# A causal attention block on one Trainium2 core: the table of interleaved jobs set anew, the inverses stored and spread ahead of the next stack

## The reference

```python
xn = _layernorm(x, axis=-1)
qkv = xn @ w_qkv.T + b_qkv                       # 16 heads of 16 channels
att = einsum('bhqd,bhkd->bhqk', q, k) / sqrt(16) + hope_bias(i - j, head)
att = softmax(where(causal, att, -inf))
attn = einsum('bhqk,bhkd->bhqd', att, v).reshape(B, T, C) @ w_proj.T + b_proj
ffn  = fp8_quantised(bf16(xn)) @ fp8_quantised(kernel)   # rounded to bf16, plus bias
out  = x + attn + ffn
```

## Time and profile before

| | us |
|---|---|
| median of three runs | 926.57 (926.45 to 929.19) |
| the profiled execution | 926.98 |
| its span, first to last instruction | 925.2 |
| PE busy | 811.6 (88%) |
| DVE busy | 716.6 (77%) |
| ACT busy | 574.8 (62%) |
| POOL busy | 527.2 (57%) |

### The profile page before, as it was taken

How to read it: one execution, slowest core, us unless ns; L and a number is a source line. 1 busy time by engine, 2 the same in 40 slices (tenths; PEclk the granted TensorE clock), 3 DMA queues, 4 the chain that set the end, 5 groups by cost and what they waited for, 6 DMA issues and landing times.

```text
span 925.2 us, 22869 instructions
## 1 busy us (share of the span) xinstructions
PE 811.6 (88%) x6121; PEld 497.2 (54%) x6121; DVE 716.6 (77%) x2523; ACT 574.8 (62%) x1194; POOL 527.2 (57%) x521
## 2 busy tenths in 40 slices
PE   7688888998998889899889898888989989899883
PEld 4455455554555555465556555555554555555442
DVE  4778678897877987888798887888787988879702
ACT  4256567676666757677666666766676776666550
POOL 5435538575573857556474765558375655738360
PEclk9669799998999999999999999999998999999786
DMA  5926455564655555555655565466456646646202
GB/s 150 173 62 117 88 120 117 121 126 106 128 118 127 112 115 126 120 121 121 140 108 112 114 141 122 110 128 120 109 122 121 128 108 129 122 99 120 56 31 76
DMA packets 55549, 106.08 MB, mean 115 GB/s; under 512 B 10464, under 2 KB 30432, under 8 KB 55520
## 3 DMA queue, kind: packets, MB, share of 16 engines
q1 hardware_dynamic: 55048, 105.19, 54.1%
q10 hardware_dynamic: 472, 0.54, 0.2%
HBM read 18.68 MB, written 8.91 MB: 30 GB/s over the span
## 4 chain that ended last, share of the span: by engine, by line
PE 56%; DVE 12%; SPq 10%; issue 7%; ACT 7%; DMA 6%; ACTq 1%; POOL 0%; DVEq 0%; POOLq 0%
PE misc_a L535 9%; PE misc_a L646 9%; PE misc_b L646 9%; PE misc_b L535 6%; PE scoreT_b L624 5%; PE scoreT_c L624 4%; ACT probs L879 4%; PE scoreT_a L624 4%; SPq L324 3%; DVE quant_work L997 3%; SPq L377 2%; DMA stacks<-neg_max_T 2%; SPq L371 2%; PE score_a L601 2%; DVE row_max L958 2%
## 5 line engine op out<-in xcount | busy, mean ns | idle before, releaser
L1174 POOL TENSOR_SCALAR_AFFINE_SELECT probs<-probs 128x512 f32<-128x512 f32 x256 | 166.7, 663 | 264.5 <-ACT probs L879 263.3
L958 DVE CUSTOM_DVE_ANT_0 score_b<-score_b,causal_mask_q 128x384 f32<-128x384 f32 (+3 forms) x321 | 162.0, 521 | 82.1 <-PE score_b L601 80.7
L958 DVE CUSTOM_DVE_ANT_0 score_c<-score_c,causal_mask_q 128x256 f32<-128x256 f32 (+3 forms) x384 | 169.8, 469 | 52.1 <-PE score_c L601 51.4
L879 ACT ACTIVATE probs<-scoreT_c 128x384 f32<-128x384 f32 (+1 forms) x256 | 135.1, 528 | 107.7 <-PE scoreT_c L624 52.9
L958 DVE CUSTOM_DVE_ANT_0 score_a<-score_a,causal_mask_q 128x512 f32<-128x512 f32 x319 | 172.5, 557 | 16.3 <-PE score_a L601 16.2
L879 ACT ACTIVATE probs<-scoreT_a 128x512 f32<-128x512 f32 (+1 forms) x256 | 141.4, 553 | 51.1 <-PE scoreT_a L624 36.5
L879 ACT ACTIVATE probs<-scoreT_b 128x384 f32<-128x384 f32 (+1 forms) x256 | 132.4, 517 | 31.3 <-PE scoreT_b L624 22.4
L958 DVE DVE_READ_ACCUMULATOR2_ANT row_max<- 128x1 f32 x1024 | 143.1, 140 | 0.0
L624 PE MATMUL scoreT_a<-stacks 64*128 64x512 f32 (+3 forms) x320 | 119.5, 393 | 26.6 <-DMA stacks<-neg_max_T 15.5
L624 PE MATMUL scoreT_c<-stacks 64*128 64x256 f32 (+3 forms) x384 | 123.6, 346 | 12.3 <-ACT probs L879 10.4
L601 PE MATMUL score_b<-stacks 64*128 64x384 f32 (+3 forms) x321 | 116.5, 395 | 11.1 <-DVE row_max L958 11.1
(11 more groups left out here) (234 smaller groups left out, 2019.1 us busy)
## 6 DMA issues: line engine op xcount, KB each, us to landing
stacks<-qk_parts SPq DMA_DIRECT2D x128, 512.0 KB, 8.1
x_ring<-in_L_attn_x SPq DMA_DIRECT2D x16, 512.0 KB, 3.4
attn<-out_T SPq DMA_DIRECT2D x64, 128.0 KB, 2.7
xn<-recips SPq DMA_DIRECT2D x31, 256.0 KB
out<-x_ring SPq DMA_DIRECT2D x15, 512.0 KB, 2.9
stacks<-neg_max_T SPq DMA_DIRECT2D x128, 4.0 KB
low_features<-neg_max_T SPq DMA_DIRECT2D x124, 4.0 KB
low_features<-probs SPq DMA_DIRECT2D x8, 128.0 KB, 4.1
```

Source lines behind the costliest of these rows:

```text
L879: A(probs_slot(g, k), STB[(SLOTS * g + k) % 3][:, 0:w], ACT.Exp).then_inc(exp_done, 1)
L958: last = V.tensor_tensor_reduce(bank, bank, CMQ[:, T - w:T], 1.0, LEAST, ALU.add, ALU.max, MX[:, g % 2, h, qt:qt + 1])
L1174: last = GP.affine_select(out=d, in_=d, compare_op=ALU.is_ge, fill=0.0, base=0, pattern=[[0, HU], [1, P]], channel_multiplier=-1)
```

## The change

The change edits the tables of slots, one ACT and one DVE step, one place in POOL's list and SP's list.

| job or step | before | after |
|---|---|---|
| PV (PE) | (g,3) | (g,3) |
| MT (PE), max_T (ACT) | (g,5), (g,6) | (g,3) behind PV, k = 4 behind out_T |
| QK jobs (PE) | (0,7) (0,9) (1,7) (1,11) | (0,8) twice, (1,8) twice |
| V jobs | (2,1) (2,11) | (2,6) twice |
| FF jobs | (2,7) twice | (2,9) twice |
| PJ jobs | (3,1) (3,7) | (3,6) twice |
| result (DVE) | (3,2) (3,8) | (3,6) (3,8) |
| XH (ACT) | (3,10) (3,11) | (3,9) (3,10) |
| XB (ACT) | (0,2) (0,3) | behind XH, (3,9) (3,10) |
| T_lo (DVE) | (0,0) (0,1) | (3,10) and (0,2) |
| invert (DVE) | (0,10) | (0,8) |
| attn_hi (ACT) | (2,7) (2,8) | (2,3) twice |
| quant_magic (DVE) | (2,7) (2,8) (2,9) | (2,3) (2,5) (2,6) |
| divide (POOL) | behind mask (1,2) | in front of it |

XB no longer waits for T_lo; T_lo now waits for XB, and a T bank counts as free once T_lo has read it. SP stores the inverses right behind `load_max(b, 1)` and spreads them behind the load of x, both ahead of `load_stack(b + 1, 0)`; before, the store stood behind that stack and the spread behind `load_max(b, 2)`.

```diff
-QK_AT = [(0, 7), (0, 9), (1, 7), (1, 11)]
+QK_AT = [(0, 8), (0, 8), (1, 8), (1, 8)]
...
@@ sync, body
                 load_max(b, 1)
+                if not first:
+                    store_recips(b - 1)
                 if load:
                     if not first:
                         sp.wait_ge(out_stored, 16 * b)
                     sp.wait_ge(x_loaded, 16 * (b + 2))
                     load_x(b + 2)
+                if not first:
+                    spread_recips(b - 1, last)
                 if not last:
                     wait_alone(sp, (w_loaded, 16), (st_ready, ROW * b + SLOTS),
                                (ql_ready, 4 * (b + 1) + 2))
                     load_stack(b + 1, 0)
-                if not first:
-                    store_recips(b - 1)
                 regroup(b, 0, first)
                 load_max(b, 2)
-                if not first:
-                    spread_recips(b - 1, last)
@@ tensor
-                return {"V": (vs_ready, 2 * b + i + 3), "T": (xb_ready, 2 * b + i + 5),
+                return {"V": (vs_ready, 2 * b + i + 3), "T": (xl_ready, 2 * b + i + 5),
...
-                        if due(MT_AT, g, k) and not (last and g == 3):
-                            job_MT(*((b, g + 1) if g < 3 else (b + 1, 0)))
                         if (g, k) == PV_AT[pg] and not (first and g == 0):
                             pv(pb, pg, first)
+                        if due([FIRST_MT_AT] if first and g == 0 else MT_AT, g, k) and not (last and g == 3):
+                            job_MT(*((b, g + 1) if g < 3 else (b + 1, 0)))
@@ scalar
             def XB_evac(b, ct):
-                act.wait_ge(xl_ready, 2 * b + ct + 1)
                 A(XB[:, ct, :], misc_of("T", ct)[:, :], ACT.Copy).then_inc(xb_ready, 1)
...
                             out_T(pb, pg, first and pg == 0)
+                            if not (last and g == 3):
+                                max_T(*((b, g + 1) if g < 3 else (b + 1, 0)))
...
                             for i in due(XH_AT, g, k):
                                 XH_evac(b + 2, i)
+                                if i == 0:
+                                    act.wait_ge(xy_ready, b + 1)
+                                XB_evac(b + 2, i)
@@ vector
             def T_lo(b, ct):
-                dve.wait_ge(xh_ready, 2 * b + ct + 1)
+                dve.wait_ge(xb_ready, 2 * b + ct + 1)
...
-                            for i in due(FIRST_XL_AT if first else XL_AT, g, k):
-                                T_lo(b + 1, i)
+                            for i in due(FIRST_XL_AT if first and g == 0 else XL_AT, g, k):
+                                if g < 3 or more:
+                                    T_lo(b + 1 if g < 3 else b + 2, i)
@@ gpsimd, body
-                    mask(b, g, 2)
                     if g == 1 and not first:
                         divide(b - 1)
+                    mask(b, g, 2)
```

48 lines of the change are left out of this document (21 added, 27 removed).

## The result

The kernel became slower, where faster was forecast: 957.09 us (median of four runs, 952.14 to 967.4) against 927.88 (926.45 to 930.09) of the kernel before on the same chip, a ratio of 1.0295 with a 95% interval of 1.0244 to 1.0345. It lies outside the range of 885 to 935. The profiled execution took 952.14 us (span 950.4). One of the four executions, 967.4 us, was in a slower state; it counts in the median but not in the ratio.

A forecast was written before the change was run, and what follows sets the result against it. PE, 88% busy, was taken as bound partly by the 12.06 us chain from stack issue to restart, a slower clock costing nothing. Terms summed to -1.45 us a turn, x 14 = -20.3 us, giving 906.5 us, range 885 to 935.

The forecast's parts named there:

- XB beside XH: PV at (0,3) no longer waits for its bank, which XB's copy still had to read: -0.92 us a turn.
- MT behind PV: MT at (0,3) waits 0.85 us for T_lo's bank; taken as +0.7 us a turn, bounds nothing and 1.4.
- SP's chain: Store and spread ahead of the stack bring PE's restart to 452.0 from 452.90: taken as -0.8 us, bounds -1.65 and +1.9.
- V before FF: The second V job no longer waits for FF's bank, with ACT reading V at (2,6): -0.63 us a turn.
- quant_magic: Its three parts fall beside PV and the V pair, when DVE has no scores: -0.5 us, bounds -0.7 and 0.
- Pairs: Paired jobs stop the scores about 3 us, giving PE new waiting from g2 to g3: +0.7 us, bounds 0 and 1.5.
- The rest: Low clock after the restart stays, T's second job still waits for RESULT: 0, bounds -0.7 and +0.5 us.
- C: Stack late: regroup taken 7.8 us after the stack's last issue gives +1.25 us a turn, 944 us; chance 0.16.
- B: DVE is the next bound: MT's move and the pairs cost 1.4 + 1.5 us, sum 0, 926 us; chance 0.16.
- The last sentence of the prediction: Wrong at the root if PE's wait for the maxima exceeds 1.65 us or turns differ with PE's clock anew.

The follow-up runs named there:

- QK single: Changed kernel with only the QK jobs and their readers back at the single slots of the kernel before; 912.4 us, ratio 0.9852.
- SP's part: Kernel before with only store and spread of the inverses ahead of the stack, invert at (0,8), divide ahead of mask (1,2); 911.0 us, ratio 0.9829.
- fillers: Constant matmuls added in slots 0 to 2: twelve a turn in the changed kernel, 966.3 us; six in the early-store kernel with QK pairs, 960.7 us.

## Why the prediction was wrong

The forecast was -1.45 us a turn; measured was +2.30. By its own steps:

1. *XB beside XH, -0.92.* The wait went, the time did not: alone +0.65 in the turn, 929.3 us. The step looked at PE's wait for its bank and not at what PE meets next, the maxima (+8.0 us) and exp (+6.1 us).
2. *MT behind PV, +0.7.* Sign right. Alone it cost 1.04 us a turn, half of it lost clock and half waits, most of these for exp, which the prediction had at nothing. The wait that it had named came too, 8.5 us in 7 waits after, and in the kernel after with QK single 16.7 us in 13 waits, 1.28 us each: near the upper bound of 1.4, not at the 0.85 chosen.
3. *SP's chain, -0.8.* Right in size (-1.08 alone), but in part by luck: the chain to the restart, from which the step was worked out, gave 0.2 to 0.4 us, and 0.67 was clock that was no longer lost. The store did issue in 0.35 us, and the regroup's first DMA was taken 4.3 us behind the stack (5.0 forecast). That its second one would block instead was not seen, and left 0.4 us of the chain's gain; the stack of the next group also comes 1.95 us earlier, which the step didn't have. In the kernel after the chain is 12.25 us (455.21 to 467.46), no shorter than before, since the regroup comes later there, behind a PV of 3.96 us.
4. *V before FF, -0.63.* The wait is gone; its worth was not measured alone. Together with the V, FF and PJ pairs it came to -1.69 in the changed kernel with QK single. The same wait also went when `attn_hi` and quant_magic came early, without any new order of V and FF.
5. *quant_magic, -0.5.* Right in size (-0.59 on SP's part), though not clear of noise, and mixed with the end of FF's wait. Where pairs are it is much more: 64.7 us between the two kernels with V, FF and PJ pairs. By the Trainium skill ("SBUF — State Buffer", section "SBUF: two separate sides") a DVE instruction with two SBUF inputs and a GpSimd one that reads SBUF lock each other out of the shared ports: whoever starts first holds them for its whole instruction. The trace's median of 0.69 and maximum of 0.76 us after, against 1.12 and 2.29 before, agrees with two engines that meet less there.
6. *Pairs, +0.7, bounds 0 and 1.5.* This is the step that failed. All pairs cost 1.86 us in the mean turn of the changed kernel and 4.79 on the kernel before; QK pairs alone 3.55 in the changed kernel and 2.36 on SP's part. Counted in waits the step was not far off (QK pairs on SP's part: +0.47). But a pair's price was counted in waits alone.
7. *The rest, "the low clock after the restart stays while a wait near 1 us stays: 0".* This is the term that was missing: +3.27 us a turn. It was taken as fixed, one fall behind the restart at g2. But the clock falls at other places too: before the change 13 of 52 PVs took over 3.3 us, five of them at (0,3), and after it 27, in up to three places of one turn.

Both errors, 6 and 7, rest on one reading: that a slower clock costs the turn nothing, since two windows of equal width had different clocks and since the chain to the restart takes 12.06 us "whatever PE does beside it". The thirteen turns of before have a mean of 52.4 us at 0.99 and 1.00 (two), 53.3 at 0.96 and 0.97 (seven) and 54.0 at 0.94 (four). The chain did hide a part: it ends in a wait of PE in eight of the thirteen turns, and of some 3.2 us of lost clock at 0.94 it gave back 1.7. That is all it had to give, and further falls lengthen the turn: after the change the turns at 0.91 and 0.85 are 3 to 6 us longer than the one at 1.00. Whole executions point the same way, loosely: in fifty executions of the kernel before, 0.01 of mean clock goes with 3 us on the average, with single ones well off (924.85 us at 0.923, 925.7 at 0.929), and the kernel after took 952.1 at 0.892, 956.3 at 0.882 and 957.9 at 0.880, 5 us for 0.01. By these two slopes the 0.036 between the clocks of the two profiled executions is an estimate of 11 to 18 of their 25.2 us.

Of the rivals none was what happened. C was the slower one and named a late stack at 944; PE's longest wait for the maxima was 1.6 us, against 2.0 before, so the stack was not what came late. B named the right parts, 2 and 6, at their upper bounds, but in waits alone, and so came to 926 at most. The last sentence of the prediction, that it would be wrong at the root if turns differed with PE's clock in a new way, is what came true.

That the clock carries the loss, and not a hidden wait, rests on the ledger and on PE's busy time (the same 6121 matmuls, 30 us longer). The mean turn less lost clock less waits is 46.3 to 47.0 us in all kernels without fillers but two: 45.6 with all pairs on the kernel before, and 47.4 with XB alone. So the change of the turn is that of lost clock plus that of waits, within 0.5 us: before to after 2.30 (3.27 - 0.54), QK pairs in the changed kernel 3.55 (4.33 - 0.39), QK pairs on SP's part 2.36 (2.10 + 0.47), MT 1.04 (0.66 + 0.52), magic -0.59 (-0.13 - 0.28). For all pairs on the kernel before it is off by 1.1 (4.79 against 4.85 + 1.06), for XB alone by 0.7 the other way. Some 0.2 to 1.2 us of the QK pairs' price stay at equal clock: at full clock the changed kernel took 52.19 us with them (one turn) and 51.0 to 52.0 without (eight). What is *not* shown is why the clock falls more often: QK pairs do it, DVE's stand behind a single job does it, and more work for PE in slots 0 to 2 lessens it. Which property of a stretch decides was not separated.

## What to carry to other kernels

- Before costing a change in an engine-bound loop, list the time of *all* turns, cut at one instruction, beside their granted clock and their largest wait. If time and clock go together, or only the wait keeps them apart, the clock is part of the price of every edit that makes PE's work uneven, even if PE's waits get shorter.
- A wait that disappears is worth its time only if what PE meets next isn't late as well; two edits here took 13 and 5 us off one wait and gained nothing. Putting the parts in one by one found 902.7 us in a change that as a whole cost 3%.
- Move blocked or long DVE work into the shadow of a stretch in which DVE has nothing to read, and not right behind one: the place of quant_magic and `attn_hi` decided here between 4.5 and 61 us for the same pairs.

## What the runs showed of the hardware that was not expected

- The mean clock of a turn takes few levels (1.00, 0.94, 0.91 and 0.85 in the kernel after), and small edits shift how often each comes: with QK pairs on SP's part all thirteen turns had 0.94, while the changed kernel swings between 1.00 and 0.85 from turn to turn of one hardware loop.
- The issue of a DMA that blocks SP behind a stack's two DMAs is not bound to one line. It went from the store (3.73 us) to L372 (2.16 us) when the store was moved, while the store alone takes 0.35 us and lands in 1.5 us. The Trainium skill ("DMA: Bandwidth & Descriptors", section "Latency and other measured facts") gives about 2 us for the fixed cost of a DMA; the landing here was shorter in all fifteen stores.
- A tiny DVE instruction can take fifteen times its shortest time: the second step of the maxima's split (128x16) takes 0.16 us at best, 0.58 in the median and 2.38 at most, in both kernels. The one of 1.77 us in the earlier trace rows ended with POOL's add; the others were not traced to POOL one by one.
